# Four scan buffers in batch 0's quarters, and tokens of x2 transposed three stretches ahead of their products

## The reference, cut to what matters

```python
x = x + tanh(g_xattn) * wkv(w, u, k=layernorm(x), v=ctx)     # (4, 1024, 1024)
x = x + tanh(g_ffn)   * ffn(layernorm(x))                    # 1024 -> 4096 -> 1024
# wkv, per channel, over the tokens t of one batch:
#   y = (p + e^(u+k) v) / (q + e^(u+k));   p, q = e^w p + e^k v, e^w q + e^k
# ffn: gelu(X W0.T + bias0) rounded to fp16, then W1.T, + bias1
```

## Time and profile before

| | us |
|---|---|
| median of 3 runs | 1927.61 (1925.88 to 1928.51) |
| the profiled execution, its own time | 1929.11 |
| its span | 1927.3 |
| PE busy | 1824.5 (95%) |
| DVE busy | 882.2 (46%) |
| ACT busy | 574.9 (30%) |
| POOL busy | 335.0 (17%) |

### The profile page before, as it was taken

How to read it: one execution, slowest core, us unless ns; L and a number is a source line. 1 busy time by engine, 2 the same in 40 slices (tenths; PEclk the granted TensorE clock), 3 DMA queues, 4 the chain that set the end, 5 groups by cost and what they waited for, 6 DMA issues and landing times.

```text
span 1927.3 us, 21556 instructions
## 1 busy us (share of the span) xinstructions
PE 1824.5 (95%) x8920; PEld 881.4 (46%) x8920; DVE 882.2 (46%) x1053; ACT 574.9 (30%) x721; POOL 335.0 (17%) x349
## 2 busy tenths in 40 slices
PE   1688699999999999999999999999999999999999
PEld 0467544444444444444444444444444444444444
DVE  8788729899347858733214776741300000000000
ACT  6748324643333434311002434420101111200000
POOL 6543202555321212100000221110000000000000
PEclk9989799999999999999999999999999999999999
DMA  7595566866664353324343452333233212223330
GB/s 272 183 317 195 202 216 239 291 229 227 223 185 169 106 178 145 131 89 137 126 154 136 144 173 104 120 131 120 89 131 125 88 50 88 88 74 101 131 120 33
DMA packets 91149, 291.97 MB, mean 151 GB/s; under 512 B 13862, under 2 KB 26150, under 8 KB 83884
## 3 DMA queue, kind: packets, MB, share of 16 engines
q1 hardware_dynamic: 83132, 177.30, 27.8%
q10 hardware_dynamic: 7920, 113.30, 16.6%
HBM read 223.41 MB, written 67.16 MB: 151 GB/s over the span
## 4 chain that ended last, share of the span: by engine, by line
PE 77%; DVE 11%; ACT 4%; issue 4%; POOL 3%; DMA 1%; SPq 0%; DVEq 0%; POOLq 0%; ACTq 0%
PE accs L1124 38%; PE accs L1102 36%; DVE S L884 3%; PE accs L1083 1%; POOL W L568 1%; DVE S L872 1%; DVE S L875 1%; DVE stats L784 1%; POOL X L544 1%; DVE front L870 1%; ACT L653 1%; DVE front L853 1%; DVE front L881 1%; DVE front L878 1%; ACT L704 1%
## 5 line engine op out<-in xcount | busy, mean ns | idle before, releaser
L1124 PE MATMUL accs<-DT,W 128*128 128x512 f16 x4096 | 888.4, 380 | 0.0
L1102 PE MATMUL accs<-XT,W 128*128 128x512 f16 x3584 | 776.0, 380 | 1.1 <-ACT XT L662 1.1
L1124 PEld LDWEIGHTS accs<-DT,W 128*128 128x128 f16 x4096 | 401.4, 98 | 489.5 <-issue 10.1
L1102 PEld LDWEIGHTS accs<-XT,W 128*128 128x128 f16 x3584 | 351.1, 98 | 425.4 <-issue 2.4
L929 DVE SCALAR_TENSOR_TENSOR xo<-e,tg,xo 128x512 f32<-128x512 f16 x64 | 50.2, 785 | 635.8 <-ACT e L720 635.8
L712 ACT ACTIVATE DT<-accs,small 128x512 f16<-128x512 f32 x224 | 154.0, 688 | 490.9 <-PE accs L1102 490.4
L720 ACT ACTIVATE e<-accs,small 128x512 f16<-128x512 f32 x64 | 43.9, 685 | 654.8 <-PE accs L1124 653.1
L884 DVE RECIPROCAL S<-front 128x512 f32<-128x512 f32 (+1 forms) x72 | 215.6, 2994 | 0.0
L544 POOL TENSOR_TENSOR X<-X,S 128x512 f32<-128x512 f32 (+1 forms) x72 | 94.0, 1305 | 492.6 <-DVE S L887 492.6
L870 DVE TENSOR_TENSOR front<-front,V 128x512 f32<-128x512 f32 (+1 forms) x72 | 45.8, 636 | 135.1 <-ACT front L653 135.1
L568 POOL TENSOR_TENSOR W<-stage,W 128x1024 f16<-128x1024 f32 x41 | 86.7, 2128 | 60.3 <-ACT stage L696 60.3
(11 more groups left out here) (92 smaller groups left out, 873.3 us busy)
## 6 DMA issues: line engine op xcount, KB each, us to landing
W<-parts_dram ACTq DMA_DIRECT2D x54, 2048.0 KB, 9.2
stage<-w_in SPq DMA_DIRECT2D x52, 512.0 KB, 5.2
parts_dram<-W SPq DMA_DIRECT2D x94, 256.0 KB, 5.2
xin<-x_in SPq DMA_DIRECT2D x32, 512.0 KB, 6.9
x_dram<-X SPq DMA_DIRECT2D x32, 512.0 KB, 3.8
xo<-x_dram SPq DMA_DIRECT2D x32, 512.0 KB, 4.2
out<-xo SPq DMA_DIRECT2D x32, 512.0 KB, 9.1
V<-vT_in SPq DMA_DIRECT2D x56, 256.0 KB, 5.2
```

The source lines that it names most:

```text
L1102: mm = nc.tensor.matmul(acc[m % BANKS], W[:, (nb // Q) % 2, part, nb % Q, P * c:P * (c + 1)], XT[:, c, HALF * half:HALF * (half + 1)], sta ...
L1124: mm = nc.tensor.matmul(acc[m % BANKS], W[:, s % 2, part, q, P * c:P * (c + 1)], DT[:, nb, HALF * half:HALF * (half + 1)], start=(nb == 0 ...
```

## The change

- The scan buffers of units 0 to 15 are four (`scan_of(n)`, the same memory cut into four quarters); a residual's end seeds unit n+4 instead of n+2 there. Halves keep two.
- tanh(g) is folded into the product with v (L870 becomes a SCALAR_TENSOR_TENSOR) and into the seeds' numerators; the last step of a unit (L887) becomes a TENSOR_TENSOR.
- SECOND goes from 25 to 22 and THIRD from 64 to 61. The transposes to token layout, the moments and norms start there; `channels_x2` and `copy_xt` come in slots 24 and 25, and 62, 63 and 64; the waits for `xt_copied` stay at slots 25 and 64.
- Units 8 to 15 and 16 to 23 get earlier slots, units 8 to 11 all at slot 1, the rest up to five slots earlier; so do their residuals.
- The prologue makes 12 weight pieces instead of 15; the other 13 of the first 25 are made in slots 0 to 21, pieces 25 to 31 in slots 33 to 49 instead of 34 to 52. The load of a piece is issued three slots behind its predecessor's slot, not one.
- x's tiles 4 to 7 are normalised by ScalarE (in slots 25, 27, 28, 30), and so are x2's tiles 0, 4 and 6, with an `offset_x2` on VectorE before each. VectorE keeps x2's tiles 1, 2, 3, 5, 7.
- In the prologue the sums of x's tile 1 come before tile 0's offset; ScalarE takes over max(w, 0) of the ramp (`grow`); the small constants are reordered; x2's tile 1 goes back through the third product bank instead of `back`, and ScalarE's copies of tiles 0 and 1 come behind `norm_x(3)`.

```diff
-SECOND, THIRD = LAG, len(EARLY)
+SECOND, THIRD = LAG - 3, len(EARLY) - 3
...
-    for i, (k, a) in enumerate(((1, 5), (1, 8), (3, 10), (3, 13), (8, 16), (8, 19), (13, 21), (13, 24))):
+    for i, (k, a) in enumerate(((1, 4), (1, 7), (1, 9), (1, 11), (7, 14), (7, 16), (12, 18), (12, 21))):
         UNIT_SLOT[CB + i], ADD_SLOT[CB + i] = k, a
-    for i, (k, a) in enumerate(((31, 36), (32, 41), (37, 46), (42, 50), (47, 55), (51, 60), (56, 63), (61, 63))):
+    for i, (k, a) in enumerate(((31, 35), (32, 40), (36, 44), (40, 48), (45, 53), (49, 56), (52, 58), (56, 60))):
...
-WITH_UNIT = ((0, 1), (2,), (3, 4), (5,), (6, 7), (8,), (9, 10), (11,))
-BEHIND = (12, 13, 14)
-PREP_SLOT = {15 + j: 1 + 2 * j for j in range(LAG - 15)}
-PREP_SLOT.update({LAG + j: 34 + 3 * j for j in range(NB - LAG)})
+WITH_UNIT = ((0,), (1,), (2,), (3, 4), (5,), (6,), (7,), (8,))
+BEHIND = (9, 10, 11)
+PREP_SLOT = {12 + j: s for j, s in enumerate((0, 1, 3, 5, 7, 9, 10, 12, 14, 16, 18, 19, 21))}
+PREP_SLOT.update({LAG + j: s for j, s in enumerate((33, 35, 37, 40, 43, 46, 49))})
...
+        def scan_of(n):
+            return S4[:, n % 4, :, :] if n < 2 * CB else S[:, n % 2, :, :]
...
+            return acc[2].bitcast(F16).rearrange("p (c t) -> p c t", c=CB) if T == 1 else back[:, :, :]
...
+                follows = {2 * CB - 4: None, 2 * CB - 3: 2 * CB, 2 * CB - 2: None, 2 * CB - 1: 2 * CB + 1}.get(
+                    n, n + 4 if n < 2 * CB else n + 2)
+                if follows is not None and follows < LAST:
                     pool.wait_ge(x2_done, n + 1)
-                    seed(n + 2)
+                    seed(follows)
...
@@ scalar
+            NORM_AT = {SECOND + 3: 4, SECOND + 5: 5, SECOND + 6: 6, SECOND + 8: 7}
...
+            def norm_x2(T):
+                act.wait_ge(offset2_done, {0: 1, 4: 2, 6: 3}[T])
+                if T:
+                    act.wait_ge(xt_done, T - 1)
+                nc.scalar.activation(xhs[T % 2], token_banks(T).rearrange("p h c -> p (h c)"), ACT.Identity,
+                                     bias=offset2[:, :], scale=rstd[:, 1, T % 2, 1:2]).then_inc(xh0_ready, 1)
...
             norm_x(2)
+            norm_x2(0)
+            norm_x(3)
             copy_xt(0)
             copy_xt(1)
-            norm_x(3)
...
-                    if K == SECOND:
-                        copy_xt(2)
-                        copy_xt(3)
-                    if K == THIRD:
-                        for T in range(HT, TILES):
-                            copy_xt(T)
+                    if K in (SECOND + 2, SECOND + 3):
+                        copy_xt(K - SECOND)
+                    if K in NORM_AT:
+                        norm_x(NORM_AT[K])
+                    for T in {THIRD + 1: (4,), THIRD + 2: (5,), THIRD + 3: (6, 7)}.get(K, ()):
+                        copy_xt(T)
+                    if K in (THIRD, THIRD + 1):
+                        norm_x2(HT + 2 * (K - THIRD))
...
@@ vector
-                nc.vector.tensor_tensor(EV, E, values, ALU.mult).then_inc(ev_done, 1)
+                nc.vector.scalar_tensor_tensor(EV, E, tg[:, 0:1], values, ALU.mult, ALU.mult).then_inc(ev_done, 1)
...
-                nc.vector.scalar_tensor_tensor(S_q[:, 0:w], EV, tg[:, 0:1], S_q[:, 0:w],
-                                               ALU.mult, ALU.mult).then_inc(y_done, 1)
+                nc.vector.tensor_tensor(S_q[:, 0:w], EV, S_q[:, 0:w], ALU.mult).then_inc(y_done, 1)
...
                         norm_x2(2)
-                        norm_x(4)
-                        stats_x(5)
+                        offset_x(4)
                         norm_x2(3)
-                        lessen_x(4)
                         for T in range(5, 8):
-                            norm_x(T)
-                            if T < 7:
-                                stats_x(T + 1)
-                            lessen_x(T)
+                            stats_x(T)
+                            offset_x(T)
+                            lessen_x(T - 1)
+                        lessen_x(7)
                     if K == THIRD:
-                        stats_x2(4)
-                        for T in range(4, 8):
-                            if T < 7:
-                                stats_x2(T + 1)
-                            norm_x2(T)
+                        for T in (4, 6):
+                            stats_x2(T)
+                            sums_x2(T + 1)
+                            offset_x2(T)
+                            moments(1, T + 1)
+                            norm_x2(T + 1)
...
@@ tensor
                     if K == SECOND:
                         tokens_x2(2)
                         tokens_x2(3)
-                        channels_x2(2)
-                        channels_x2(3)
+                    if K in (SECOND + 2, SECOND + 3):
+                        channels_x2(K - SECOND)
                     if K == THIRD:
                         tokens_x2(4)
-                        for T in range(4, 8):
-                            if T < 7:
-                                tokens_x2(T + 1)
-                            channels_x2(T)
+                        tokens_x2(5)
+                    if K in (THIRD + 1, THIRD + 2):
+                        channels_x2(K - THIRD + 3)
+                        tokens_x2(K - THIRD + 5)
+                    if K == THIRD + 3:
+                        channels_x2(6)
+                        channels_x2(7)
```

## The result

The changed kernel takes 1909.85 us (median of 4 runs, 1909.24 to 1910.57), the kernel before on the same chips 1927.84: a ratio of 0.9908, with a 95% interval of 0.9891 to 0.9926, or 18.0 us less. I had forecast 1913.5 and a range of 1905 to 1923.

A forecast was written before the change was run, and what follows sets the result against it. TensorE's products bound all behind slot 64, so time follows its start, 244.5 us: VectorE or ScalarE bounds most earlier stages. A lead of 14.5 (5.5 + 6.5 + about 2.6) gave 1913.5 us, range 1905 to 1923.

The forecast's parts named there:

- Start of the prologue, hand-over: Up to group 0: unit 0 starts 1.35 us earlier, at 14.0; group 0 at 64.7, 0.6 later, behind `norm_x(3)`.
- Slots 0 to 21: ScalarE sets the pace: its work from 64.7 ends at 116.4, with seven table loads and no extra drain.
- SECOND: Tokens of x2's tiles 2 and 3 start at 116.9, 3.8 us earlier, held by GpSimd's order; group 25 at 127.05.
- Unit 16: First half unit starts at 141.65, 5.5 us earlier, after slot 30's norm, lessen, transposes, table load and exponential.
- Units 16 to 23: Half units run without the 6.5 us of gaps, blamed on pieces behind residuals on GpSimd; end 208.7, not 220.7.
- Rival (d): Slower: GpSimd's order between slots 31 and 60 makes exponentials late; gaps of 23.6 us, 1936; chance 0.05.
- THIRD: Last unit to slot 64: ScalarE's norms beside VectorE's and groups filling the chain give about 2.6 us.
- The sum: Lead at slot 64 of 14.5 us: 5.5, plus 6.5 of gaps, plus about 2.6 at THIRD.
- the clock at THIRD: After TensorE's idle stretch until 210.1: half clock for the tokens and part of group 61; slot 64 at 230.
- low clock only after 201: Sign of being right: slot 64 near 230 us, with TensorE's clock low only after 201.

The follow-up runs named there:

- e5: Changed kernel with ScalarE's copies of x2's tiles 0 and 1 ahead of its norm of x's tile 3; 1911.28 us, ratio 0.9916.
- e11: Changed kernel with three more pieces in the prologue's pause, those copies ahead of `norm_x(3)`, and residual 15 at slot 19; 1903.41 us, ratio 0.9877.
- e6: Changed kernel with the residual of unit 15 at slot 19, not 21; 1905.95 us, ratio 0.9894.
- e1: Changed kernel with two scan buffers again in the quarters, not four; 1908.99 us, ratio 0.9908.
- a0_again: The changed kernel run again without any edit, as the anchor of the set; 1910.45 us, ratio 0.9910.
- e9: Changed kernel with x's tiles 4 to 7 normalised by VectorE again, in the order of the kernel before; 1912.54 us, ratio 0.9926.
- e10: Changed kernel with units 16 to 23 and their residuals in their old slots and THIRD at 64; 1909.48 us, ratio 0.9904.
- e8: Changed kernel with pieces 25 to 31 back in their old slots, 34 to 52; 1912.38 us, ratio 0.9926.
- e3: Changed kernel with THIRD back at slot 64 in one piece, norms still shared; 1910.58 us, ratio 0.9913.
- e13: Changed kernel with all four of x2's norms at THIRD on VectorE; 1909.06 us, ratio 0.9900.
- e12: Kernel of e11 with the residuals of units 13, 14 and 15 at slots 15, 16 and 17; 1903.68 us, ratio 0.9876 to the kernel before.

## Why the prediction held

**Start of the prologue, hand-over.** Right: 13.87 for 14.0, and 64.67 for 64.7. The step that read against the change, `norm_x(3)` ahead of the copies, was the right one to look at: e5 takes it back and gets 3.1 us at group 0.

**Slots 0 to 21.** Right, the sum and that ScalarE sets the pace: its last piece there ended at 116.2 for 116.4, with seven table loads at 1.3 each. e5 and e11 show that this sum is the pace. By the rule of the Trainium skill ("ScalarE: Activation LUTs", What ACT_TABLE_LOAD costs), 1.38 us more for each switch, it would have ended near 126, an estimate from that page's figure; the measurement decides against the rule.

**SECOND.** Right in what sets the tokens: GpSimd's order (116.25 for 116.9; e6), with the end of unit 15 hidden (e1). Group 25 at 127.13 for 127.05 is luck, two errors that cancel. The tokens came 0.65 us earlier than I said, and from there to group 25 I had 10.15 us with TensorE at full clock; it took 10.9, because the clock fell behind the pause of 2.6 us that my own walk contained. Where it did not fall, in a0_again, it took 9.8, and group 25 started at 125.90, 1.15 earlier than forecast. I treated x's four norms as nothing but time taken from VectorE; e9 shows 1.3 us at unit 16 by their place ahead of the norm of x2's tile 3.

**Unit 16.** 1.1 us earlier than forecast. I let ScalarE's table load start behind the transposes. The load starts at 138.32, the transposes only at 139.05. With SECOND's clock kept (a0_again) unit 16 starts 2.4 us earlier than forecast, at 139.27.

**Units 16 to 23.** Right in size: no gap, 67.1 us. The cause I gave, pieces behind residuals on GpSimd, is right in place (e10: the old slots of the units make no gap; e8: the old slots of the pieces make one), but what e8 shows is another road than the late exponential that I had: a piece late on GpSimd holds back the residual, and with it the seed of the unit two further on. Rival (d), late units by GpSimd's order, needed gaps above 18.4 us, and there were none.

**THIRD.** Here the cause that I gave is wrong. I gave 2.6 us to ScalarE's norms beside VectorE's and to groups that fill the chain; the stage lost 3.8 us (23.8 to 20.0), but not by these: THIRD at 64 is as fast (e3), and so are all norms on VectorE (e13). What e3 and e13 still have in common, and the kernel before has not, is the order in pairs on VectorE. Before, the norm of tile 5 stood behind the statistics of tile 6, and the norm of tile 6 behind those of tile 7. VectorE's view of the kernel before shows it:

```profile
227.50 1.34 DVE L831 TENSOR_SCALAR xh<-front,mv,rstd 128x1024 f16<-128x1024 f32 x1
231.68 1.30 DVE L784 BATCH_NORM_STATS2 stats<-front 128x6 f32<-128x512 f32 x2 [2.83 <-PE front L1040]
...
233.34 1.34 DVE L831 TENSOR_SCALAR total<-front,mv,rstd 128x1024 f16<-128x1024 f32 x1
237.52 1.30 DVE L784 BATCH_NORM_STATS2 stats<-front 128x6 f32<-128x512 f32 x2 [2.84 <-PE front L1040]
```

Two idle stretches of 2.8 us, each with a norm behind it whose operands were ready. In the changed kernel the two waits of that kind are 0.5 and 1.35 us. A higher clock is not the cause: in e3 TensorE does the tokens of tile 6 in 1.91 us, at half clock as in the kernel before (1.04 in the changed kernel; those of tile 7 in 1.17), and the stage takes 20.3 us all the same. That the order in pairs is the whole gain is argued, not tried by itself. On the clock at THIRD I was right: 0.50 behind the pause, 0.76 from 212 to 214, 1.00 from 214 to 226. My sign "low clock only after 201" did not hold: besides SECOND's fall the view gives 0.72 from 180 to 185.

**The sum.** I said 14.5 us; 18.0 came (18.7 in the profiled spans): 1.1 more at unit 16, 1.3 at THIRD (20.0 for 21.3), and 1.8 behind slot 64, for which I had nothing. This last is luck and for the most part the clock: two falls fewer (3.4 us) and 1.0 us more of half clock at slot 64, which leaves 0.6 us unexplained. That the change does not bring it shows in e3 and e10, which hold most of the change and have the two falls. Of the 16.9 us at slot 64, undoing one part at a time gives 6.5 to 7.2 for SECOND ahead, 3.1 for the earlier pieces and 1.7 for x's norms on ScalarE; four buffers, THIRD ahead, the units' slots and x2's norms at THIRD give 0.4 us or less each, or cost a little. If the parts add up, some 5 us are in no run that undoes a part, and the 3.8 of THIRD belong there.

## What to carry over

Where several engines hand work to each other in fixed orders, add up what each engine has to do between two events before valuing a wait: the one whose sum fills the stage sets the pace, and a wait removed on another ends in its queue (8.2 us earlier on VectorE became 4.4 here). A late small step (a residual, a power) behind a long one that nobody needs yet is worth a look in every queue: moving one number gave 1.1 us, and the norms of x's tiles ahead of x2's cost 1.3. Work moved into an idle stretch of the engine that sets the pace gave about 4 of e11's 6.3 us, by difference. Differences of under 2 us should be read in the traces, from the start of a stage, and between profiles whose clock did the same up to there: against a profile with a fall, e9 seemed to cost next to nothing and e6 to give nearly twice what it does.

## What the runs showed of the hardware

- A table load of ScalarE is not held by the wait of the activation behind it. In the changed kernel, ahead of unit 16, it starts 0.7 us before the transposes that the exponential waits for. ScalarE in order of time:

```profile
138.32 1.28 ACT L679 ACT_TABLE_LOAD   x1
139.75 0.66 ACT L679 ACTIVATE front<-front,shift 128x512 f32<-128x512 f32 x1
```

- TensorE's clock can fall to half behind a pause of 2.0 us and stay up behind one of 2.1 us, and of ten profiles with a pause of 2.5 to 2.7 us at the same place four show a fall. Two profiles of the same kernel differ in this at two places (118 us and 530 us).
- The granted clock of the view stays at 1.00 ahead of its first fall, also where the matmuls take twice the time: sixteen in 3.60 us at group 0, thirty-two in 3.66 us later (e12, at 108.49).
